# Gated delta rule on one core: a partition half stands for a batch instead of a head

## The reference, cut to what matters

```python
decay = where(tril, exp(g[:, None] - g[None, :]), 0)
M = where(stril, (k * beta) @ k.T * decay, 0)
T = inverse(eye + M)                       # 64 x 64 per chunk
v_c, k_cumdecay = T @ (v * beta), T @ (k * beta * exp(g))
# in order over the 8 chunks of a sequence, state is 128 x 128 per value head
attn  = (q @ k.T) * decay
v_new = v_c - k_cumdecay @ state
out   = (q * exp(g)) @ state + attn @ v_new
state = state * exp(g_last) + (k * exp(g_last - g)).T @ v_new
```

## Time and profile before

| | |
|---|---|
| median of 3 runs | 2246.31 us (2246.26 to 2247.7) |
| profiled execution: its time | 2245.33 us |
| its span | 2243.5 us |
| mean granted clock of TensorE | 0.993 |
| instructions | 76444 |
| DMA over the span | 87.45 MB, mean 39 GB/s |

### The profile page before, as it was taken

How to read it: one execution, slowest core, us unless ns; L and a number is a source line. 1 busy time by engine, 2 the same in 40 slices (tenths; PEclk the granted TensorE clock), 3 DMA queues, 4 the chain that set the end, 5 groups by cost and what they waited for, 6 DMA issues and landing times.

```text
span 2243.5 us, 76444 instructions
## 1 busy us (share of the span) xinstructions
PE 2167.4 (97%) x32208; PEld 1663.8 (74%) x32208; DVE 1642.4 (73%) x3307; ACT 1308.2 (58%) x3141; POOL 1712.8 (76%) x1774
## 2 busy tenths in 40 slices
PE   3799999999999999999999999999999999998998
PEld 2677777777877777777877777778777777776654
DVE  6777777778777777778777777778777777786322
ACT  2665656665666556665666566666666566654211
POOL 2788888889888888888888888888888888898200
PEclk9899999999999999999999999999999999999999
DMA  2211101111111101111111101111111101111100
GB/s 87 63 42 37 47 20 37 38 47 33 35 48 38 48 14 43 38 47 33 35 47 38 37 20 47 38 47 33 35 47 38 33 24 47 38 38 44 39 19 19
DMA packets 70950, 87.45 MB, mean 39 GB/s; under 512 B 16720, under 2 KB 39376, under 8 KB 70608
## 3 DMA queue, kind: packets, MB, share of 16 engines
q1 hardware_dynamic: 70608, 82.55, 14.2%
HBM read 77.45 MB, written 5.08 MB: 37 GB/s over the span
## 4 chain that ended last, share of the span: by engine, by line
PE 78%; ACT 10%; DVE 5%; issue 3%; POOL 3%; DMA 1%; SPq 0%; POOLq 0%; DVEq 0%; ACTq 0%
PE ps_p L680 10%; PE ps_two L431 9%; PE ps_state L431 9%; PE ps_two L456 8%; PE ps_p L617 4%; ACT qg L804 3%; PE ps_p L505 3%; PE ps_p L590 3%; PE ps_state L641 3%; PE ps_state L505 3%; PE ps_p L625 2%; PE ps_p L456 2%; PE ps_p L738 2%; ACT L795 2%; PE ps_two L541 2%
## 5 line engine op out<-in xcount | busy, mean ns | idle before, releaser
L1415 POOL TENSOR_SCALAR Kg<-idx_s,lutb 128x134 f32<-128x134 int32 x480 | 356.9, 746 | 27.0
L1376 POOL TENSOR_TENSOR Sd<-St,el 128x512 f32<-128x512 f32 x192 | 201.5, 1049 | 221.6 <-DVEq L1273 221.6
L1252 DVE TENSOR_SCALAR Vn<-ps_p,bR 128x128 f32<-128x128 f32 x512 | 170.3, 350 | 181.7 <-PE ps_p L590 108.4
L680 PE MATMUL ps_p<-w_o,hT 128*128 128x256 f32 x1000 | 246.2, 389 | 7.3 <-ACT V L843 5.8
L1033 DVE SCALAR_TENSOR_TENSOR cacc<-ps_state,cw,cacc 128x1022 f32<-128x1022 f32 (+2 forms) x192 | 244.3, 1272 | 7.1 <-ACT cacc L771 2.3
L1033 DVE SCALAR_TENSOR_TENSOR cacc<-ps_two,cw,cacc 128x1022 f32<-128x1022 f32 (+2 forms) x192 | 245.0, 1276 | 5.3 <-DVE cacc L1033 0.5
L431 PE MATMUL ps_state<-xnT,w_qkv 128*128 128x256 f32 x1024 | 233.3, 381 | 5.9 <-DVEq L1038 5.9
L431 PE MATMUL ps_two<-xnT,w_qkv 128*128 128x256 f32 x1024 | 235.9, 384 | 0.0
L936 ACT ACTIVATE P<-ps_p 128x128 f32<-128x128 f32 x256 | 67.4, 278 | 261.0 <-PE ps_p L595 261.0
L431 PEld LDWEIGHTS ps_state<-xnT,w_qkv 128*128 128x128 f32 x1024 | 193.0, 191 | 32.3 <-DVEq L1038 6.3
L680 PEld LDWEIGHTS ps_p<-w_o,hT 128*128 128x128 f32 x1000 | 183.6, 191 | 43.6 <-issue 19.6
(11 more groups left out here) (199 smaller groups left out, 5407.1 us busy)
## 6 DMA issues: line engine op xcount, KB each, us to landing
qg<-g_scratch SPq DMA_DIRECT2D x64, 512.0 KB, 7.3
g_st<-g_scratch SPq DMA_DIRECT2D x64, 256.0 KB, 5.6
w_qkv<-in_wqkvz SPq DMA_DIRECT2D x16, 512.0 KB, 3.8
w_z<-in_wqkvz SPq DMA_DIRECT2D x16, 256.0 KB, 3.3
w_o<-in_wout SPq DMA_DIRECT2D x16, 256.0 KB, 2.9
idx_s<-in_idx SPq DMA_DIRECT2D x32, 67.0 KB, 1.9
fw_scratch<-looked_up SPq DMA_DIRECT2D x32, 67.0 KB, 2.7
Kg<-in_x SPq DMA_DIRECT2D x2, 1024.0 KB, 5.7
```

Source lines behind the costliest of these rows:

```text
L680: m = pe.matmul(bank[:, b * D:(b + 1) * D], hT[:, t, b, 1 - a, :], w_o[:, a, :], start=(a == 0), stop=(a == RATIO - 1))
L1252: dve.tensor_scalar(Vn[:, cur, b], bank[:, 0:P], bR[:, R.par, b, c:c + 1], None, ALU.mult).then_inc(done, 1)
L1376: pool.tensor_tensor(Sd[:, :, :, :], St[:, c % 2, :, :, :], el[:, R.par, :, :, c].unsqueeze(3).broadcast_to([P, BB, RATIO, P]), ALU.mult). ...
L1415: m = pool.tensor_scalar(slots[k], idx_s[:, :], float(k), lutb[:, k:k + 1], ALU.is_equal, ALU.mult)
```

## The change

The two halves of the partitions are now the two batches of a pair, and the two value heads lie side by side. The keys of both batches stand one above the other in `kq[:, c, 0, half, :]`, so that

- `kkq` is computed once for both heads, batch by batch with 64 columns of weights, 16 matmuls in two banks (they were 16 with 128 columns in four); `U` is formed from it by two operations of 128 x 512 in place of four of 128 x 256, and the minus sign moves into `nbR`;
- `kt` takes 8 transposes in two banks in place of 16 in four, and goes to `kt`, from which POOL forms both `Kg` and `Kd`; scores go to `qk`, from which POOL forms `A`;
- ACT writes the keys once (before, twice), and scales the values in 8 operations of 256 elements in place of 16 of 128, all of them in `begin`, where half of them stood in `invert`;
- DVE needs one operation for the squared lengths of a bank in place of four; gates per chunk stay in `sct` on the chip, and the way through DRAM (`sc_dram`) and its two loads a round go.

Beside this, the second output quarter moves in front of level 4 (`range(2 if R.nxt else 3)`), the third into the place that the second had, and projection 5 from beside the second products of level 4 to beside the first products of level 5, where the third quarter stood. On DVE quarter 0 is added before the taps of kind 0, and quarter 1 before those of kind 1.

```diff
-PROJ_AT = {(4, 1): (4, 5), (5, 1): (6, 7)}
-OUT_AT = {(4, 0): (1,), (5, 0): (2,), (5, 1): (3,)}
+PROJ_AT = {(4, 1): (4,), (5, 0): (5,), (5, 1): (6, 7)}
+OUT_AT = {(4, 0): (2,), (5, 1): (3,)}
...
-    begin = (spread([("kkq", i) for i in range(4)], (4, 5, 6, 7)) + spread([("kt", i) for i in range(4)], (4, 5, 7, 6))
-             + spread([("vt", i) for i in range(4)], (1, 7, 4, 5)))
+    begin = (spread([("kkq", i) for i in range(2)], (4, 5)) + spread([("kt", i) for i in range(2)], (6, 7))
+             + spread([("vt", i) for i in range(4)], (1, 4, 5, 7)))
...
             def begin(R):
 
                 pe.wait_ge(s["silu"], R.at(0, 4, 4))
-                for i in range(4):
+                for i in range(2):
                     bank, filled = wait_open(pe, R, "kkq", i)
                     for u in range(4):
-                        c = (i % 2) * 4 + u
-                        m = pe.matmul(bank[:, u * P:(u + 1) * P], kq[:, i // 2, c, 0:P], kq[:, i // 2, c, C:3 * C],
-                                      start=True, stop=True)
+                        for half in range(2):
+                            m = pe.matmul(bank[half * C:(half + 1) * C, u * P:(u + 1) * P], kq[:, i * 4 + u, 0, half, :],
+                                          kq[:, i * 4 + u, :, half, :], start=True, stop=True)
                     m.then_inc(filled, 1)
-                for i in range(4):
+                for i in range(2):
                     bank, filled = wait_open(pe, R, "kt", i)
...
                 if R.before() is not None:
-                    for t in range(1 if R.nxt else 3):
+                    for t in range(2 if R.nxt else 3):
                         outputs(R, "out", R.before(), t)
...
             def begin(R):
-                for i in range(4):
-                    act.wait_ge(s["u_c"], R.at(i + 1, 0, 4))
+                for i in range(2):
+                    act.wait_ge(s["u_c"], R.at(i + 1, 0, 2))
...
-                    act.activation(A[:, b, c4, :], src[:, :, C:P], ACT.Copy).then_inc(read[n], 1)
-                for i in range(4):
-                    copy_turned(R, "kt", i, Kd)
+                    act.activation(qk[:, i * 4:i * 4 + 4, :], src[:, :, C:P], ACT.Copy).then_inc(read[n], 1)
+                for i in range(2):
+                    bank, done = wait_full(act, R, "kt", i)
+                    act.activation(kt[:, i * 4:i * 4 + 4, :], bank[:, :].rearrange("p (c t) -> p c t", t=P), ACT.Copy
+                                   ).then_inc(done, 1)
                 act.wait_ge(s["rinv_c"], R.at(0, 1, 1))
                 values(R, 0)
+                values(R, 1)
...
             def sums(bank, dst, scale, more):
 
-                for odd in range(2):
-                    src = bank[odd * C:(odd + 1) * C, 0:BB * NC // 2 * WIDE].rearrange("p (b c w) -> p b c w", b=BB, w=WIDE)
-                    for a in range(RATIO):
-                        to = dst[a * C:(a + 1) * C].rearrange("p b (c two) -> p b c two", two=2)[:, :, :, odd]
-                        dve.tensor_scalar(to, src[:, :, :, 0], scale, more, ALU.mult, ALU.add
-                                          ).then_inc(s["n2_c"], 1)
+                src = bank[:, 0:NC * WIDE].rearrange("p (c w) -> p c w", w=WIDE)[:, :, 0]
+                dve.tensor_scalar(dst, src, scale, more, ALU.mult, ALU.add).then_inc(s["n2_c"], 1)
...
-                for i in range(4):
-                    if i == 2 and last is not None:
+                for i in range(2):
+                    bank, _ = wait_full(dve, R, "kkq", i)
+                    c4 = slice(i * 4, i * 4 + 4)
+                    src = bank[:, :].rearrange("p (c t) -> p c t", t=P)[:, :, 0:C]
+                    dve.tensor_tensor(U[:, :, c4, :], DB[:, :, c4, :], src.unsqueeze(1).broadcast_to([P, RATIO, 4, C]), ALU.mult
+                                      ).then_inc(s["u_c"], 1)
+                    if i == 0 and last is not None:
                         gated(last, 2)
...
-                if R.nxt:
-                    taps(R, 0, (1, 2, 3))
                 if of is not None:
                     for t in range(1 if R.nxt else 3):
                         outputs(R, "out", of, t)
+                if R.nxt:
+                    taps(R, 0, (1, 2, 3))
                 second_products(R, 4, 2)
                 turn()
+                if R.nxt and of is not None:
+                    outputs(R, "out", of, 1)
```

More of the change, by code:

```diff
@@ L249, in wait_read, with scalars @@
             eng.wait_ge(read[n], 1 + m + 1)
+        def scalars(k, par, h):
+            return sct[:, k, par, :, h, :].rearrange("p c a -> p a c")
         def rounds(eng, body):
@@ L302, in load_wz, with load_round @@
                 sp.dma_start(w_z[:, :, :], wqkvz[:, :, bass.ds(h * HW + 4 * HD, 2 * HD)]).then_inc(s["ld_wz"], 16)
[L304 to L308, removed]
-                                 ).then_inc(s["ld_round"], 16)
-            def load_rows(h, par):
+            def load_round(h, par):
                 b0 = par * BB
@@ L441, in lengths @@
                     wait_open(pe, R, "n2", i)
-                per = BB * NC // parts
-                for n in range(part * per, (part + 1) * per):
-                    b, c, odd = n // NC, n % NC, n % 2
-                    m = pe.matmul(bank[odd * C:(odd + 1) * C, n // 2 * WIDE:(n // 2 + 1) * WIDE],
-                                  sqk[:, i * BB + b, c * C:(c + 1) * C], ones[:, 0:WIDE], start=True, stop=True)
+                per = NC // parts
+                for c in range(part * per, (part + 1) * per):
+                    for half in range(2):
+                        to = half if i else 1 - half
+                        sq = flat(sqk)[:, (i * NC + c) * P + half * C:(i * NC + c) * P + (half + 1) * C]
+                        m = pe.matmul(bank[to * C:(to + 1) * C, c * WIDE:(c + 1) * WIDE], sq, ones[:, 0:WIDE],
+                                      start=True, stop=True)
                 if part == parts - 1:
@@ L666, in turn_back @@
                 bank, filled = wait_open(pe, *place_of_turn(R, i))
[L667 removed]
+                dst = bank[:, :].rearrange("p (a b s t) -> p s a b t", a=RATIO, b=BB, t=C)
                 for u in range(4):
[L669 removed]
+                    m = pe.transpose(dst[:, u // 2, u % 2], on[:, i, u * P:(u + 1) * P], ident)
                 m.then_inc(filled, 1)
@@ L835, in begin, with values @@
                 values(R, 0)
-            def values(R, b):
-                for i in range(2 * b, 2 * b + 2):
+                values(R, 1)
+            def values(R, n):
+                for i in range(2 * n, 2 * n + 2):
                     bank, done = wait_full(act, R, "vt", i)
-                    for u in range(4):
-                        c = (i % 2) * 4 + u
-                        m = act.activation(V[:, b, c, :], bank[:, u * P:(u + 1) * P], ACT.Copy,
-                                           scale=rinv[:, b, c:c + 1])
+                    for u in range(2):
+                        c = i * 2 + u
+                        m = act.activation(V[:, :, c, :], bank[:, u * 2 * P:(u + 1) * 2 * P].rearrange("p (a t) -> p a t", t=P),
+                                           ACT.Copy, scale=rinv[:, c:c + 1])
@@ L849, in invert @@
                     tap0(R, 0)
-                values(R, 1)
                 if R.nxt:
@@ L1222, in invert @@
                     hidden(1, 1, AHEAD[1])
-                if R.nxt and of is not None:
-                    outputs(R, "out", of, 1)
                 second_products(R, 5, 4)
@@ L1270, in recur @@
                             else:
-                                dve.tensor_tensor(dst, Sd[:, b, :, :], part, ALU.add).then_inc(s["st_c"], 1)
+                                dve.tensor_tensor(dst, Sd[:, :, b, :], part, ALU.add).then_inc(s["st_c"], 1)
                         dve.wait_ge(s["st_c"], R.at(2 * c + 2, 0, 2 * (NC - 1)))
```

183 lines of the change are left out of this document (86 added, 97 removed).

## The result

The changed kernel takes 2289.56 us (median of 4 runs, 2286.61 to 2290.47), the kernel before 2246.28 us beside it: ratio 1.019, 95% interval 1.0173 to 1.0208. It is slower, by 43 us; 20 were forecast. That is inside the range, and at the value of the rival in which the clock falls in every round (2290).

What follows compares the result with a forecast made beforehand. PE's own instruction stream was taken as the bound. From 2246.3 us: +3 for 30 ordinary rounds, -2 for round 0, -5 for the last round, +24 for the clock, giving 2266 us; 8-in-10 range 2226 to 2290.

Steps and rivals of the forecast that it cites:

- the rival in which the clock falls in every round: PE's clock falls behind the stand in all 30 ordinary rounds: 48 us, hence 2290 us; chance 0.10.
- the stand: PE idle before level 5's second products, waiting for ACT's copy of the first products: some 1.9 us per round.
- the fourth turn's wait: Fourth turn of the values, moved to bank 7, waits for ACT's copy of the second key turn: +0.4 us per round.
- Term 7: Level 5's second products wait for ACT's copy, queued behind tap 0, which waits for projection 5: +1.95 us per round.
- So I take a fall in half of the rounds.: Behind the stand PE's clock falls in 15 of 30 rounds, at 1.6 us each: +24 us.
- term 8: DVE's small copies of squared lengths fall from eight to two, with one new negation: -0.1 us per round.
- the ends: Round 0 saves 2 us on key products and key writes; the last round saves 5 us as V is made ahead.
- term 3: Two new tile-shape switches between 128-column transposes and 64-column key products: +0.1 us per round (0 to 0.2).
- the rival's 0.54: Each tile-shape switch empties the array, two times 0.27 us per round: 2280 us; chance 0.05.
- term 1's far bound: Key products: each pair of 64-column instructions costs what one 128-column instruction did, saving 1.8 us per round.
- "No wait" at level 4: PE reaches level 4 16.4 us after the key products began, W is there at 15.4, so no wait.
- The rival without a stand: No stand arises before level 5's second products: 58 us more won, clock stays up, 2184 us; chance 0.08.

Runs made afterwards that it cites:

- order_alone: The kernel before with only the new order of projections, output quarters and DVE additions, old layout kept: 2326.39 us, ratio 1.0351.
- fill_half: The changed kernel with two unread 256-column matmuls per round in PE's stand before level 5's second products: 2255.54 us, ratio 1.0035.
- copy_first: The changed kernel with ACT's copy of level 5's first products put ahead of its tap-0 copy: 2227.41 us, ratio 0.9909.
- less_dve_new: copy_first without DVE's addition of the second output quarter, that part left out of the output: 2209.92 us, ratio 0.9834.
- late_work: The changed kernel with one more 256-column matmul per round behind level 5's second products: 2290.0 us, ratio 1.0192.
- layout_alone: The changed kernel's new layout with the old order of projections, output quarters and taps: 2269.09 us, ratio 1.0094.

## Why the prediction was off

**What held.** The sign; the stand, its place, its releaser and its size (1.94 us against 1.95); the fourth turn's wait (0.32 against 0.4); 8 turns. The wait for V in the last round fell from 5.8 to 1.6 us. Term 7, in order_alone, came to 2.1 us a round, though taking the stand away there won only 0.8.

**The step that failed: "So I take a fall in half of the rounds."** 25 of 30 rounds fell. With a price of 1.4 us each (forecast 1.6) that is 34 us in place of 24. It is one of two parts of about equal size: of the 23 us between 2266 and 2290 it makes some 10, and the base, below, the rest. I had two cases from round 0, a stand that was followed by a fall (after a second one of 1.3) and a single one of 1.26 that was not, and took a half between them. I also took the first one for shorter than it was: 92.5 to 94.3 is a window inside the stand, not the stand. The timeline of PE in the kernel before has

```profile
94.43 0.24 PE L486 MATMUL ps_p<-XW,U 64*64 64x32 f32 x1 [2.05 <-DVE XW L1182]
```

so the stand was 2.05 us. The new one of 1.95 lies 0.1 under it and 0.7 over the one without a fall. The case nearest to it had fallen, and the rival with a fall in each round should have had more than 0.10. fill_half agrees with the other end: after 1.1 us no round falls.

**The second step that failed: the base was 12 us too low.** Without the clock 2242 was forecast and 2254 measured. About 2 us of it come from terms 1 to 7, 6 from term 8, and 6 from the ends; that is 14, but these are differences of single traces, in which the start of round 0 alone lies anywhere from 75.4 to 78.3 us.
- Key products saved 1.68 and turns (1.13 us for 8) 0.89 us in the round shown, together 2.57 against 2.45 forecast; in the others 8 turns take 0.93 us, and the two save 2.77.
- The changes of tile shape (term 3, 0.1) can be seen. Behind the last key product the first turn starts 0.2 us later where a turn follows a turn after 0.11, and the next one takes 0.06 more. In front of the key products stand four turns of the output. Before, with the same shape behind them, they took 1026.60 - 1026.11 = 0.49 us, now 1048.92 - 1048.33 = 0.59:

```profile
1026.11 0.66 PE L669 MATMUL ps_two<-cst,on 128*128 128x128 f32 x4
```

  That is 0.1 in front and 0.15 behind, and the first pair of key products takes 0.05 more than the others: 0.3 in all, above the term's range but under the rival's 0.54. The key products hide it: behind their first pair two instructions come every 0.109 us, where one did before every 0.112, which was term 1's far bound.
- "No wait" at level 4 failed by 0.15 us: that wait is there in 28 of 30 rounds, and it is one of the prediction's own signs of being wrong. W came at 15.98 us after the key products and not at 15.4: U starts 1.57 us after them, and the blocks operation took 1.26 us in the round shown (1.59 in the mean), as POOL's ran beside it.
- Not in the sum at all: projection 4 waits 0.34 us for DVE, 10 us in all. I followed ACT's order and PE's, and not what the quarter put ahead of DVE's taps does to the banks that the taps free.
- Until the second products of level 5 the round is 0.28 us later than before (0.20 forecast); behind them it loses another 0.1 where 0.1 was to be won.
- The ends gave 1 us, not 7. Round 0 began 0.9 us later and took 0.6 longer (64.87 against 64.25), with one fall more in it. Behind the key products of round 31 2.7 us were won, not 5: the wait for V is 4.2 shorter, but PE waits 1.8 for W.

**The rival without a stand was mispriced.** It had 30 x 1.95 us won on PE. copy_first won 0.9 a round: with the stand gone, the sum of DVE's operations between two rounds' U and last taps is the bound, and less_dve_new shows it. My first paragraph called the condition "as long as no other engine is late" thin in two places; it was thin along all of DVE's stream, which I never summed.

**Open.** What decides in which rounds the clock falls. Under a stand of 1.94 us it was 25, 17 and 10 of 30 in three kernels whose undisturbed rounds take 63.7, 64.0 and 65.4 us, so the stand's length alone does not set it. The order in time that late_work's traces show speaks for the place of the stand in time, but no run here varied the round's length alone.

## What to carry to other kernels

When an engine's stream is cut, add up the next engine's operations between two fixed points of the round before pricing the gain: the saving ends there, and a stand that is taken away gives back only the difference. A stand of PE of about 2 us can cost more through the clock than by itself (34 us here, beside the 27 that went with it when copy_first took it away), and moving one copy ahead of an operation that waits for something else removes both. After work has moved in time, compare the mean duration of unchanged operations: one that doubled had slid under another engine's, and one wait moved on GpSimd won it back.

## What the runs showed of the hardware

- Standing 1.9 us per round, PE was given the lower clock in 25, 24, 17 or 10 rounds of 30 (changed, layout_alone, late_work, order_alone); standing 1.1 us, in none. Useless matmuls in the stand made the kernel 34 to 35 us faster.
- 32 key instructions with 64 columns of weights, in alternating column halves, took 1.90 us, 0.059 each; with 128 columns 0.112 each. The step from 128-column turns to them cost 0.1 us, the step back 0.15.
- An operation of DVE with two SBUF inputs (128 x 512) took 0.77 us in the mean with GpSimd's multiplication held back and 1.59 beside it, ending 0.55 us after GpSimd's whenever it had begun.
